# Two-layer attention network on one core: the last network's weights split earlier, and GpSimd's sums in whole slots

## The chip, the cores and the metric

The kernel runs on one core of one Trainium2 chip. The time is the device time of one execution in microseconds (us), and the figure shown for a kernel is the median of its runs. The core has five engines that take their instructions in order, each from its own queue: PE (TensorE, matmuls; its weight loads are shown apart as PEld), DVE (VectorE), ACT (ScalarE), POOL (GpSimd) and SP (SyncE, which here only issues transfers). They wait for each other by semaphores: an instruction adds to one when it is done, and another engine's queue stands at a wait until the count is reached.

## The reference, cut to what matters

Two layers, each an attention times a gate, on 2 sequences of 1024 tokens with 128 features. The change lies in the second layer.

```python
# layer 2: x is (2, 1024, 128), 16 heads of 64
xn = rms_norm(layernorm(x), gamma)
q, k, v = split(xn @ w_qkv)
attn = softmax(q @ k.T * 64**-0.5)          # per head
s = concat(attn @ v) @ w_out
h = silu((ln @ w1) * s1) * ((ln @ w2) * s2) # "last network", 512 wide; ln = layernorm(x)
h = gelu((h @ h1) * sh1)
h = gelu((h @ h2) * sh2)
x = x + s * silu((h @ w3) * s3)
```

## The kernel before

**The second attention** runs in 16 steps, m = 0 to 15. A step is one sequence and one pair of heads. It has 16 slots: two halves of 512 queries, and in each half 8 tiles of 128 keys. A slot works on both heads of the pair, so its probabilities `prob` are 128x1024 (two heads by 512 queries). Slots come in batches b = 0 to 7 of two. PE makes the scores of a slot (`st_ps`, lines 1691 to 1703), ACT takes the exponential into one of 6 `prob` buffers (L1862), PE multiplies it with the values (`o_ps`, L1719). The kernel also needs the sum of the probabilities over the keys: POOL adds slot after slot into `acc` (L2053), one operation for each head, 7 slots of each half (the first slot is an operand of the second). The two operations of a slot are independent of each other; each waits only for the same head's operation of the slot before.

When a half's sums are complete, DVE transposes them (`turned`, L1952) and reduces them (`den_part`, L1959), PE and ACT sum over partitions (`den_out`), DVE takes the reciprocal and spreads it (`rden`, L1967) and multiplies the half's output with it (`o_n`, L1975, an operation with both inputs in SBUF). PE then projects `o_n` (`pj_ps`, L1624) and DVE adds the result to `y` (L1915). `o_n` of a step's second half is made in batch 5 of the next step, that of the first half in batch 7 of its own. Between these DVE takes the row maxima of the next step (`mx_part`, L1924 and L1927), which frees the PSUM banks into which PE writes the next products.

**The order** of each engine is written out by hand in the functions `tensor`, `scalar`, `vector`, `gpsimd` of `second_attention` (called for every m and b, or every slot) and in the blocks at the end of `two_layers`. After step 15 the calls with m = STEPS (16) finish it: PE has its last values' products (slots 14, 15), then the last network begins.

**The last network** uses fp32 operands split into a high and a low part. Its weights are 14 tiles: m1 and m2 (128x512 each), four of h1, four of h2 (128x512), four of m3 (128x128). `scalar_split` makes the high part on ACT (L2226), `gpsimd_split` the low part on POOL (L2231). The raw weights are loaded by SP (`sync_raw`) behind step 3. `splits_at` says which tile is split when: one tile in each of steps 8 to 13 (in batch 4 on ACT, behind slot 9 on POOL), and the other 8 in step 15, where POOL does them behind its last slot. The high parts lie over `xr`, the tokens of the attention's projections, so that half of them can be made only when the first sequence is through and half only when the last projection is done; the input's split (`x_hi`, `x_lo`) is done in step 15 too, on POOL behind slot 10.

## Time and profile before

| | |
|---|---|
| median of 2 runs | 1076.24 us (1076.05 to 1076.44) |
| the profiled execution's own time | 1075.95 us |
| its span, first to last instruction | 1074.2 us |
| PE busy in the span | 1042.9 us, 97% |
| POOL busy | 822.9 us, 77% |
| DVE busy | 801.8 us, 75% |
| ACT busy | 564.3 us, 53% |
| PE of the 40 slices of the span, busy tenths | 9 in all but two: slice 35 has 4, the last 8 |
| chain that ended last, by engine | PE 74%, DVE 11%, POOL 6%, issue 5%, ACT 3% |

The whole-span shares hide the stages. The second attention's steps run from about 300 to 925 us, the last network from about 945 us to the end. A timeline row is a run of like instructions on one engine: start, duration, line, names, shapes, count, and in brackets how long the engine was idle before it and what released it. A record of POOL can begin shortly before the one ahead of it has ended.

### The profile page before, as it was taken

What the parts mean: (1) busy time and instruction counts of PE and PEld (TensorE: products, weight loads), DVE (VectorE), ACT (ScalarE), POOL (GpSimd) and SP (SyncE); (2) the same over time, 40 slices, a digit from 0 to 9 for tenths busy, and PEclk for the clock granted to TensorE, in tenths of its full rate; (3) what the DMA queues carried; (4) which work ended last, traced back from release to release, by engine and by line L of the source; (5) the groups of instructions that cost most, each with busy time, mean ns of one, the idle gap of its engine ahead of it and who ended that gap; (6) DMA issues with size and microseconds to landing.
All of it is one profiled execution on the core that took longest, in us unless ns stands there. A gap on an engine that the chain in (4) does not pass through costs nothing.

```text
span 1074.2 us, 22406 instructions
## 1 busy us (share of the span) xinstructions
PE 1042.9 (97%) x8784; PEld 666.2 (62%) x8784; DVE 801.8 (75%) x1235; ACT 564.3 (53%) x912; POOL 822.9 (77%) x742
## 2 busy tenths in 40 slices
PE   9999999999999999999999999999999999499998
PEld 7898898777645545545554545555554554167886
DVE  4657866577767878878888887888787886965553
ACT  4634453556565555556555565555555555334442
POOL 5778997755469999999999999999999999900000
PEclk9999999999999999999999999999999999799999
DMA  7423234543000000300000000000000000000000
GB/s 231 140 81 100 85 121 125 163 133 115 23 1 2 1 2 1 108 1 1 2 1 1 2 1 1 2 1 1 2 1 2 1 2 1 0 1 10 10 1 20
DMA packets 32681, 40.24 MB, mean 37 GB/s; under 512 B 4544, under 2 KB 24384, under 8 KB 31296
## 3 DMA queue, kind: packets, MB, share of 16 engines
q1 hardware_dynamic: 32256, 38.80, 11.0%
q8 instruction: 70, 1.15, 0.4%
q14 instruction: 35, 0.29, 0.1%
q10 hardware_dynamic: 320, 0.01, 0.0%
HBM read 28.97 MB, written 9.70 MB: 36 GB/s over the span
## 4 chain that ended last, share of the span: by engine, by line
PE 74%; DVE 11%; POOL 6%; issue 5%; ACT 3%; SPq 0%; DMA 0%; DVEq 0%; POOLq 0%; ACTq 0%
PE o_ps L1719 15%; PE mx_ps L1672 6%; PE ha_banks L641 4%; PE st_ps L1691 4%; PE st_ps L1697 4%; PE st_ps L1694 4%; POOL acc L2053 4%; PE bank L2142 4%; PE bank L2143 3%; PE bank L2144 3%; PE pj_ps L1624 2%; PE mx_ps L1604 2%; PE mx_ps L1609 2%; DVE o_n L1975 2%; DVE mx_part L1924 2%
## 5 line engine op out<-in xcount | busy, mean ns | idle before, releaser
L2053 POOL TENSOR_TENSOR acc<-acc,prob 128x512 f32<-128x512 f32 x384 | 491.2, 1320 | 9.3 <-ACT prob L1862 9.3
L1862 ACT ACTIVATE prob<-st_ps 128x1024 f32<-128x1024 f32 x256 | 248.4, 1022 | 208.5 <-PE st_ps L1697 106.6
L1719 PE MATMUL o_ps<-prob,v_cur 128*64 128x512 f32 x1024 | 244.8, 599 | 0.0
L1924 DVE TENSOR_REDUCE mx_part<-mx_ps 128x1 f32<-128x512 f32 x258 | 168.2, 679 | 28.5 <-PE mx_ps L1672 17.5
L1719 PEld LDWEIGHTS o_ps<-prob,v_cur 128*64 128x64 f32 x1024 | 69.6, 137 | 122.1 <-issue 82.4
L1927 DVE TENSOR_REDUCE mx_part<-mx_ps 128x2 f32<-128x1024 f32 x78 | 95.5, 1225 | 45.4 <-PE mx_ps L1672 45.3
L1672 PE MATMUL mx_ps<-k_hi,q_hi 64*128 64x512 f32 x414 | 112.0, 456 | 2.5 <-DVE mx_part L1927 0.4
L1697 PE MATMUL st_ps<-q_hi,d_lo 64*128 64x512 f32 x512 | 101.8, 390 | 0.0
L2053 POOL TENSOR_TENSOR acc<-prob 128x512 f32<-128x512 f32 x64 | 80.9, 1285 | 26.1 <-ACT prob L1862 26.1
L1672 PEld LDWEIGHTS mx_ps<-k_hi,q_hi 64*128 64x128 f32 x414 | 47.0, 183 | 84.2 <-issue 51.2
L949 POOL TENSOR_TENSOR ha_wide<-ha_pt,ha_own 128x512 f32<-128x512 f32 x64 | 74.5, 1188 | 9.2 <-ACT ha_pt L905 9.1
L1691 PE MATMUL st_ps<-q_hi,d_hi 64*128 64x512 f32 x384 | 76.9, 392 | 0.0
L1694 PE MATMUL st_ps<-q_lo,d_hi 64*128 64x512 f32 x384 | 76.4, 390 | 0.0
L1975 DVE TENSOR_TENSOR o_n<-o_sum,rden 128x512 f32<-128x512 f32 x32 | 60.4, 1888 | 0.1
L1924 DVE TENSOR_REDUCE mx_part<-pj_ps 128x1 f32<-128x512 f32 x86 | 58.4, 679 | 0.0
L1697 PEld LDWEIGHTS st_ps<-q_hi,d_lo 64*128 64x128 f32 x512 | 49.0, 184 | 10.3
L2260 ACT ACTIVATE whole<-bank,cols 128x512 f32<-128x512 f32 x32 | 22.0, 688 | 61.9 <-PE bank L2144 61.9
L1624 PE MATMUL pj_ps<-o_n,wo 128*64 128x512 f32 x128 | 33.9, 609 | 15.5 <-DVE o_n L1975 15.5
L1604 PE MATMUL mx_ps<-xr,w_raw 128*64 128x512 f32 x168 | 45.3, 618 | 0.0
L1835 ACT ACTIVATE o_sum<-o_ps 128x512 f32<-128x512 f32 x32 | 19.2, 600 | 47.5 <-PE o_ps L1719 47.5
L1952 DVE STREAM_TRANSPOSE turned<-acc 128x1024 f32<-128x1024 f32 x32 | 39.5, 1235 | 4.8 <-POOL acc L2053 4.8
L861 ACT ACTIVATE ha_q<-ha_banks,ha_head_bq 128x128 f32<-128x128 f32 x128 | 35.5, 377 | 12.5 <-PE ha_banks L641 12.5
(392 smaller groups left out, 2159.4 us busy)
## 6 DMA issues: line engine op xcount, KB each, us to landing
w_tile<-w_rows SPq DMA_DIRECT2D x72, 128.0 KB, 3.0
v_rows<-ha_v SPq DMA_DIRECT2D x8, 1024.0 KB, 4.1
ha_vt<-v_rows SPq DMA_DIRECT2D x16, 512.0 KB, 4.1
q_max<-mx_turned SPq DMA_DIRECT2D x128, 1.0 KB
h_w<-in_h SPq DMA_DIRECT2D x2, 1024.0 KB, 8.3
w_raw<-in_w SPq DMA_DIRECT2D x8, 192.0 KB, 3.9
head_wkv<-in_wkv SPq DMA_DIRECT2D x2, 512.0 KB, 4.8
m_w<-in_m SPq DMA_DIRECT2D x3, 256.0 KB, 3.0
```

Source lines behind the costliest of these rows:

```text
L949: d = pool.tensor_tensor(wide[r][:, seq, :, :, :], t.unsqueeze(3).to_broadcast([P, G // 2, HEADS, GROUPS]), own[:, :].unsqueeze(1).unsquee ...
L1604: mm = pe.matmul(to[rows(h), :], w_raw[:, p, of], xr[:, chunk(q, half), :], start=True, stop=True, skip_group_check=True)
L1672: mm = pe.matmul(to[h], q_hi[q % 2][rows(h), tile(i)], k_hi[q % 2][rows(h), half_of(keys)], start=True, stop=True)
L1691: pe.matmul(st[:, h, :], upper[rows(h), :], qh[rows(h), half_of(half)], start=fresh, stop=False, skip_group_check=True)
L1694: pe.matmul(st[:, h, :], upper[rows(h), :], ql[rows(h), half_of(half)], start=False, stop=False, skip_group_check=True)
L1697: mm = pe.matmul(st[:, h, :], dl[rows(h), tile(j)], qh[rows(h), half_of(half)], start=False, stop=not fresh, skip_group_check=True)
L1719: mm = pe.matmul(o_ps[rows(h), :], v_cur[:, m % 2, j, rows(h)], prob[:, (16 * m + slot) % RING, h, :], start=(j == 0), stop=(j == KT - 1), ...
L1862: act.activation(prob[:, n % RING, :, :], st_ps[:, slot % 2, :, :], ACT.Exp, scale=SCALE).then_inc(s_exp, 1)
L1924: dve.reduce_max(mx_part[:, h, i, keys:keys + 1], maxima_banks(q, n)[h], AX_X).then_inc(s_mxr, 1)
L1927: dve.reduce_max(mx_part[:, :, i, keys:keys + 1], both, AX_X).then_inc(s_mxr, 1)
L1975: dve.tensor_tensor(o_n[:, half, :], o_sum[:, half, :], rden[:, half, :], ALU.mult).then_inc(s_on, 1)
L2053: pool.tensor_tensor(total, old, new, ALU.add).then_inc(s_acc, 1)
```

## The change

1. POOL adds both heads of a slot in one 128x1024 operation (was two of 128x512). It now waits for the operation of the slot before, its immediate predecessor, and counts 2 on `s_acc`.
2. In step 15 POOL stops after slot 11. The last four slots are added by DVE, in `vector_add`, behind DVE's work of step 15.
3. In step 15 POOL waits, before slot 10, until `s_on` has reached 30, that is until DVE has made `o_n` of step 14's second half.
4. The high parts of the weights lie in free memory. So the splits run one tile a step from step 3 (steps 3 to 12), the four small tiles of m3 together in step 13, and none in step 15. SP loads the raw weights behind step 1 (was 3).
5. The input's split moves to step 14: batch 2 on ACT, behind slot 7 on POOL. The waits for the projections go.

```diff
+    BY_VECTOR = 12
...
+    def vector_add(dve, slot):
+        dve.wait_ge(s_exp, 16 * (STEPS - 1) + slot + 1)
+        dve.wait_ge(s_acc, 2 * (ADDS * (STEPS - 1) + 7 + slot - KT - 1))
+        dve.tensor_tensor(acc[:, 1, :, :], acc[:, 1, :, :], prob[:, (16 * (STEPS - 1) + slot) % RING, :, :], ALU.add)\
+           .then_inc(s_acc, 2)
...
-        if j == 0:
+        if j == 0 or m == STEPS - 1 and slot >= BY_VECTOR:
             return
+        if (m, slot) == (STEPS - 1, BY_VECTOR - 2):
+
+            pool.wait_ge(s_on, 2 * m)
         if j == 1 and m:
             pool.wait_ge(s_turns, den_done(m - 1, half, "turned"))
         pool.wait_ge(s_exp, 16 * m + slot + 1)
-        for h in range(2):
-            new, total = prob[:, (16 * m + slot) % RING, h, :], acc[:, half, h, :]
-            old = prob[:, (16 * m + slot - 1) % RING, h, :] if j == 1 else total
-            if j > 1:
-                pool.wait_ge(s_acc, 2 * (ADDS * m + 7 * half + j - 2) + h + 1)
-            pool.tensor_tensor(total, old, new, ALU.add).then_inc(s_acc, 1)
+        new, total = prob[:, (16 * m + slot) % RING, :, :], acc[:, half, :, :]
+        old = prob[:, (16 * m + slot - 1) % RING, :, :] if j == 1 else total
+        if j > 1:
+            pool.wait_ge(s_acc, 2 * (ADDS * m + 7 * half + j - 1))
+        pool.tensor_tensor(total, old, new, ALU.add).then_inc(s_acc, 2)
...
-            act.wait_ge(t2.s_pj, t2.V_HALF)
-        if i == EARLY:
-            act.wait_ge(t2.s_pj, t2.V_END)
...
-        LOADED = 3
+        LOADED = 1
...
-        SPLIT_END = 4
+        FIRST_SPLIT, WIDE = 3, end.TILES - HT
         def splits_at(m, b):
-            if m == END:
-                return [end.EARLY + 2 * b, end.EARLY + 2 * b + 1] if b < SPLIT_END else []
-            return [m - PAIRS] if b == 4 and 0 <= m - PAIRS < end.EARLY else []
+            n = m - FIRST_SPLIT
+            if b != 4 or not 0 <= n <= WIDE:
+                return []
+            return [n] if n < WIDE else range(WIDE, end.TILES)
...
-                        if m == END and b == SPLIT_END:
+                        if (m, b) == (END - 1, 2):
                             end.scalar_x(act)
...
+                for slot in range(t2.BY_VECTOR, 16):
+                    t2.vector_add(dve, slot)
                 t2.vector(dve, STEPS, 0)
...
-                        if m == END and slot == 2 * SPLIT_END + 2:
+                        if (m, slot) == (END - 1, 7):
                             end.gpsimd_x(pool)
-                        if m < END and slot % 2:
+                        if slot % 2:
                             for i in splits_at(m, slot // 2):
                                 end.gpsimd_split(pool, i)
-                for i in range(end.EARLY, end.TILES):
-                    end.gpsimd_split(pool, i)
```

On POOL, the end of its queue: step 15 and what follows, in the kernel before (`acc<-prob` is a half's first add, `h_lo` and `m_lo` are weight splits, `x_lo` the input's).

```order
L2053 TENSOR_TENSOR acc<-prob 128x512 x2
L2053 TENSOR_TENSOR acc<-acc,prob 128x512 x12
L2053 TENSOR_TENSOR acc<-prob 128x512 x2
L2053 TENSOR_TENSOR acc<-acc,prob 128x512 x2
L2277 TENSOR_TENSOR x_lo<-xn,x_hi 128x512
L2053 TENSOR_TENSOR acc<-acc,prob 128x512 x10
L2231 TENSOR_TENSOR h_lo<-h_w,h_hi_200 128x512
```

Three more `h_lo` and the four `m_lo` of m3 follow it.

The same place after the change: steps 14 (from its first half's last adds) and 15.

```order
L2063 TENSOR_TENSOR acc<-acc,prob 128x1024 x6
L2277 TENSOR_TENSOR x_lo<-xn,x_hi 128x512
L2063 TENSOR_TENSOR acc<-prob 128x1024
L2063 TENSOR_TENSOR acc<-acc,prob 128x1024 x2
L2044 TENSOR_TENSOR d_lo<-d_all,d_hi 128x768
L2063 TENSOR_TENSOR acc<-acc,prob 128x1024 x4
L2063 TENSOR_TENSOR acc<-prob 128x1024
L2063 TENSOR_TENSOR acc<-acc,prob 128x1024 x6
L2063 TENSOR_TENSOR acc<-prob 128x1024
L2063 TENSOR_TENSOR acc<-acc,prob 128x1024 x2
```

The eight splits behind step 15 are gone, `x_lo` is in step 14, and POOL's work ends with slot 11.

On DVE, from `den_part` of step 15's batch 5 to the last network's first operation, before.

```order
L1959 TENSOR_REDUCE den_part<-turned 128x32
L1975 TENSOR_TENSOR o_n<-o_sum,rden 128x512
L1965 RECIPROCAL den_rcp<-den_out 128x16
L1967 STREAM_TRANSPOSE rden<-den_rcp 128x512
L1975 TENSOR_TENSOR o_n<-o_sum,rden 128x512
L1915 TENSOR_TENSOR y<-pj_ps,y 128x512
L2301 SCALAR_TENSOR_TENSOR whole_217<-bank,cols,sgm_244 128x512
```

The same place after the change (line 1982 is the new add).

```order
L1960 TENSOR_REDUCE den_part<-turned 128x32
L1976 TENSOR_TENSOR o_n<-o_sum,rden 128x512
L1966 RECIPROCAL den_rcp<-den_out 128x16
L1968 STREAM_TRANSPOSE rden<-den_rcp 128x512
L1976 TENSOR_TENSOR o_n<-o_sum,rden 128x512
L1982 TENSOR_TENSOR acc<-acc,prob 128x1024 x4
L1916 TENSOR_TENSOR y<-pj_ps,y 128x512
L2301 SCALAR_TENSOR_TENSOR whole_217<-bank,cols,sgm_244 128x512
```

Only the row with the four adds is new; they stand between the second `o_n` and `y`. PE's order is the same in both kernels.

## Rows read from the trace of the kernel before

**Rows 1.** Windows: stretch, its length; busy us (count) by engine; PE clock; DMA
```profile
core 0: us, PE busy (x) PEld busy (x) DVE busy (x) ACT busy (x) POOL busy (x), PEclk, DMA share, GB/s
430.00:480.00 50.00, 49.73 (x330) 25.59 (x328) 42.15 (x64) 27.05 (x37) 47.99 (x38) 1.00 0.17 59
...
547.39:586.94 39.55, 39.41 (x268) 20.28 (x266) 33.58 (x50) 22.06 (x29) 37.47 (x30) 1.00 0.01 1
...
744.11:783.66 39.55, 39.41 (x267) 20.29 (x266) 32.29 (x50) 22.51 (x30) 38.73 (x31) 1.00 0.01 1
...
925.10:945.60 20.50, 4.98 (x12) 1.39 (x12) 17.63 (x5) 0.91 (x2) 14.82 (x15) 0.58 0.00 1
945.60:1000.00 54.40, 54.40 (x239) 42.62 (x238) 33.61 (x55) 24.32 (x38) 0.00 (x0) 1.00 0.02 6
```

**Rows 2.** Chain that ended last, in order of time: the same instruction, a step apart
```profile
547.12 1.25 DVE mx_part L1924 x2
...
586.66 1.25 DVE mx_part L1924 x2
```

**Rows 3.** Timeline of PE at the end of step 15 and after
```profile
923.15 1.94 PE L1719 MATMUL o_ps<-prob,v_cur 128*64 128x512 f32 x8
940.62 1.98 PE L1624 MATMUL pj_ps<-o_n,wo 128*64 128x512 f32 x4 [15.53 <-DVE o_n L1975]
...
945.62 0.50 PE L2142 MATMUL bank<-x_hi,m_hi 128*128 128x512 f32 x1
...
951.31 1.08 PE L1624 MATMUL pj_ps<-o_n,wo 128*64 128x512 f32 x4
```

**Rows 4.** Timeline of DVE, same stretch
```profile
915.24 1.25 DVE L1952 STREAM_TRANSPOSE turned<-acc 128x1024 f32<-128x1024 f32 x1 [4.83 <-POOL acc L2053]
...
917.66 22.82 DVE L1975 TENSOR_TENSOR o_n<-o_sum,rden 128x512 f32<-128x512 f32 x1
...
941.51 0.69 DVE L1975 TENSOR_TENSOR o_n<-o_sum,rden 128x512 f32<-128x512 f32 x1
...
947.45 0.75 DVE L2301 SCALAR_TENSOR_TENSOR whole<-bank,cols,sgm 128x512 f32<-128x512 f32 x1 [4.06 <-ACT sgm L2249]
```

**Rows 5.** Timeline of POOL, step 15 and its splits
```profile
897.72 2.52 POOL L2053 TENSOR_TENSOR acc<-prob 128x512 f32<-128x512 f32 x2
900.19 14.94 POOL L2053 TENSOR_TENSOR acc<-acc,prob 128x512 f32<-128x512 f32 x12
...
938.19 1.74 POOL L2231 TENSOR_TENSOR m_lo<-m_w,m_hi 128x128 fp32r<-128x128 f32 x4
```

**Rows 6.** Timeline of DVE in batches 5 to 7 of step 6
```profile
565.51 1.33 DVE L1975 TENSOR_TENSOR o_n<-o_sum,rden 128x512 f32<-128x512 f32 x1
...
568.48 0.69 DVE L1924 TENSOR_REDUCE mx_part<-mx_ps 128x1 f32<-128x512 f32 x1 [0.34 <-PE pj_ps L1672]
...
573.60 1.68 DVE L1975 TENSOR_TENSOR o_n<-o_sum,rden 128x512 f32<-128x512 f32 x1
576.42 1.23 DVE L1927 TENSOR_REDUCE mx_part<-mx_ps 128x2 f32<-128x1024 f32 x1 [1.15 <-PE mx_ps L1672]
```

**Rows 7.** Timeline of POOL, step 6, slot 10
```profile
563.78 5.45 POOL L2053 TENSOR_TENSOR acc<-acc,prob 128x512 f32<-128x512 f32 x4 [0.64 <-ACT prob L1862]
```

**Rows 8.** Lines by form, POOL: names, shapes, count, busy us, mean ns, idle before
```profile
L2053 POOL TENSOR_TENSOR acc<-acc,prob 128x512 f32<-128x512 f32 x384 | 491.2, 1320 | 9.3 <-ACT prob L1862 9.3
...
L2036 POOL TENSOR_TENSOR d_lo<-d_all,d_hi 128x768 fp32r<-128x768 f32 x16 | 29.2, 1828 | 1.6 <-ACT d_hi L1829 1.6
...
L985 POOL TENSOR_TENSOR head_wkv_lo<-head_wkv,head_wv_hi 128x1024 fp32r<-128x1024 f32 x1 | 2.4, 2393 | 4.9 <-ACT head_wv_hi L884 4.9
```

**Rows 9.** Timeline of POOL: L481 waits for the completion of L477, its predecessor
```profile
35.71 0.22 POOL L477 CAST wc_hi<-wc_raw 128x32 fp32r<-128x32 f32 x1
36.01 0.46 POOL L481 TENSOR_TENSOR wg_lo<-wg_raw,wg_hi 128x128 fp32r<-128x128 f32 x1
```

**Rows 10.** Lines by form, DVE: a two-input operation on 256 columns
```profile
L1902 DVE TENSOR_TENSOR d_lo<-pj_ps,k_hi 128x256 fp32r<-128x256 f32 x15 | 6.4, 424 | 15.0 <-ACT k_all L1811 15.0
```

**Rows 11.** Timeline of ACT: the last exponentials of step 15
```profile
922.57 1.94 ACT L1862 ACTIVATE prob<-st_ps 128x1024 f32<-128x1024 f32 x2 [1.51 <-PE st_ps L1697]
```

More of the change, by code:

```diff
@@ L2061, in second_attention @@
     s.vector_normalize = vector_normalize
+    s.vector_add, s.BY_VECTOR = vector_add, BY_VECTOR
     s.vector_start, s.gpsimd_start, s.gpsimd_begin = vector_start, gpsimd_start, gpsimd_begin
@@ L2065, in second_attention, with last_network @@
     s.s_osum, s.s_out = s_osum, s_out
-    s.V_END, s.V_HALF = count_of[STEPS - 1, ("v", 1)], count_of[PAIRS - 1, ("v", 1)]
+    s.V_END = count_of[STEPS - 1, ("v", 1)]
     s.ADDS_END, s.MXR_END = 2 * ADDS * STEPS, MXR_END
     return s
-def last_network(nc, c, e, t2, a, x, xn, out, raw, at, token_places, weight_place, pair_place, raw_place, late_place):
+def last_network(nc, c, e, t2, a, x, xn, out, raw, at, free_place, spare_place, weight_place, pair_place, raw_place, late_place):
     s = Const()
-    w_hi = {"h1": [token_places[i // 2][0].sb(f"h1_hi{i}", [P, HID], F32R) for i in range(HT)],
-            "h2": [token_places[i // 2][1].sb(f"h2_hi{i}", [P, HID], F32R) for i in range(HT)],
-            "m1": [token_places[2][0].sb("m1_hi0", [P, HID], F32R)], "m2": [token_places[2][0].sb("m2_hi0", [P, HID], F32R)],
-            "m3": [token_places[2][1].sb(f"m3_hi{i}", [P, P], F32R) for i in range(HT)]}
+    w_hi = {n: [free_place.sb(f"{n}_hi{t}", [P, size], F32R) for t in range(of)] for n, (of, size) in MLP_W.items() if n != "h2"}
+    w_hi["h2"] = [spare_place.sb(f"h2_hi{t}", [P, HID], F32R) for t in range(HT)]
     w_lo = {n: weight_place.sb(n + "_lo", list(t.shape), F32R) for n, t in raw.items()}
-    x_hi, x_lo = (pair_place.sb(n, [P, CH], F32R) for n in ("x_hi", "x_lo"))
+    x_hi, x_lo = (spare_place.sb(n, [P, CH], F32R) for n in ("x_hi", "x_lo"))
     RING = 3
@@ L2104, in last_network @@
     cut_by = {n: max(i for i, (of, _) in enumerate(tiles) if of == n) + 1 for n in raw}
-    EARLY = cut_by["h1"]
     USES = 2 * HT + 2 * HT
@@ L2269, in scalar_x @@
     def scalar_x(act):
-        act.wait_ge(t2.s_pj, t2.V_END)
-        act.wait_ge(t2.s_st, 16 * (STEPS - 1))
         act.activation(x_hi[:, :], xn[:, 0, HALO:], ACT.Copy).then_inc(s_xhi, 1)
@@ L2335, in vector_last @@
             dve.tensor_tensor(fin[:, of], x[:, k, of], res[:, of], ALU.add).then_inc(s_fin, 1)
-    s.TILES, s.EARLY = len(tiles), EARLY
+    s.TILES = len(tiles)
     s.sync_raw, s.sync_out = sync_raw, sync_out
@@ L2404, in two_layers @@
         WEIGHTS = late.at
-        token_places = [[Region(nc, XR + 8 * KB * i + 4 * KB * half) for half in range(2)] for i in range(3)]
-        end = last_network(nc, c, e, t2, a, x, xn, out, raw, at, token_places, Region(nc, WEIGHTS), Region(nc, HEAD + 56 * KB),
-                           Region(nc, HEAD + 91 * KB), Region(nc, FIRST))
+        end = last_network(nc, c, e, t2, a, x, xn, out, raw, at, Region(nc, XR + 8 * KB), Region(nc, pairs.at), Region(nc, WEIGHTS),
+                           Region(nc, HEAD + 56 * KB), Region(nc, HEAD + 91 * KB), Region(nc, FIRST))
         BATCHES, TURNS = t2.BATCHES, head.TURNS
```

## The prediction

> **What bounds the kernel now.** I read the page first (PE busy almost throughout, one thin slice near the end), then the windows, the chain, and the timelines of three engines at the thin slice. A step takes 39.54 us: the same DVE instruction of the chain comes back after 586.66 - 547.12 [rows 2]. In such a step PE is busy 39.41 of 39.55 us, so the attention is paced by PE, and POOL, with 37.47 us in a step without a split and 38.73 us in one with a split, follows closely behind it [rows 1]. Behind 945.6 us PE is busy without a break [rows 1]. The one hole is between: from 925.1 to 945.6 us PE is busy 4.98 of 20.50 us [rows 1]. It waits 15.53 us for `o_n` of step 14's second half, then starts again slowly: the projection takes 1.98 us where the same four matmuls take 1.08 us at 951.31 [rows 3]. The granted clock of that stretch is 0.58 on average, between the two levels of 1.2 and 2.4 GHz, and 1.00 behind it [rows 1].
>
> Why is `o_n` late? The operation is not waiting for data that comes late in POOL's work; it is recorded as running, for 22.82 us, where the same operation takes 0.69 us at 941.51 [rows 4]. It starts at 917.66 and ends at 940.48. POOL has a record at every moment from 897.72 on and ends at 939.93, 0.55 us earlier [rows 5]. So I read it as DVE standing at a port that POOL never lets go. In step 6 the same operation takes 1.33 and 1.68 us [rows 6]: there POOL gives way after the add that is running. The difference in step 15 is that POOL runs behind and has its whole queue ready. Its consecutive records overlap: 14 adds take 897.72 to 915.13, 1.24 us each, less than one's mean duration of 1.32 us [rows 5, 8].
>
> **The change part by part.**
>
> *The hole.* PE's last products of slots 12 and 13 run 923.15 to 925.09, then comes the projection of `o_n`, then the products of slots 14 and 15, then the last network, which started at 945.62 [rows 3]. If `o_n` is there in time, this is 1.94 + 1.08 + 1.94 us behind 923.15, less about 0.1 us that rows overlap: the network starts at 928.05. That gives 945.62 - 928.05 = 17.57 us, the idle time of 15.53 us and 2.0 us of slow clock. PE's order is unchanged and it is busy throughout behind that, so the shift is carried to the end, unless DVE or POOL is late for it.
>
> *When is `o_n` ready?* First the price of a double add on POOL. The trace has one POOL operation of two inputs on 1024 columns, 2.39 us; 512 columns take 1.32 us with waits in it and 768 take 1.83 us [rows 8], so 1024 by the slope from 512 to 768 is 2.34 us. I take 2.39. The new wait for its own predecessor costs a gap: where POOL waits so already, one record ends at 35.93 and the next begins at 36.01, 0.08 us [rows 9]. So a slot costs 2.47 us, against 14.94/6 = 2.49 us for its two adds before [rows 5]: merging neither gains nor loses. The bound below is 2.34 + 0.08 = 2.42, above two single durations and the gap, 2 x 1.32 + 0.08 = 2.72 us.
>
> In step 15 the first half's sums start at 897.72 [rows 5]; `x_lo`, new in step 14, finds some 2 us of idle time there. They end at 897.72 + 2.39 + 6 x 2.47 = 914.9 us (915.1 before). DVE reaches `o_n` 2.42 us after it begins to transpose them (917.66 - 915.24 [rows 4]), at 917.4. POOL does slot 9 until 917.3 and then stands at the new wait for `s_on`. Behind it in POOL's queue are slots 10 and 11 only. So the port is free, `o_n` takes 0.69 us and is done by 918.2, 6.9 us before PE wants it at 925.09.
>
> *The last four slots.* POOL does slots 10 and 11 from 918.3 to 923.2, or 923.9 if DVE's second `o_n` slips in between. DVE's adds have two inputs of 1024 columns, which no row shows. 256 columns take 0.42 and 512 take 0.69 us [rows 10, 4], so 1024 by the slope take 1.23 us; the bound above is POOL's 2.39 us. I take 1.23, the same engine's slope, and 0.08 us for each wait: 4 x 1.31 = 5.2 us, to 929.1 us. The probabilities are there at 924.5 [rows 11]. DVE's `y` add ends at 929.8, and its first operation of the last network, at 947.45 before [rows 4], is wanted at 929.88. It just fits. With 2.39 us an add the chain would be 4.6 us late. That DVE is late by less than a microsecond costs nothing; the rest would go into the time, so up to 4 us for this bound.
>
> *The splits.* Ten of the fourteen tiles now run in steps 3 to 12, one each, a window in which PE has no hole to hide them. POOL pays 38.73 - 37.47 = 1.26 us a step [rows 1], inside the 39.55 us that PE takes, and in steps like that at 744.11 PE was busy as before. What ACT pays hides in an engine that is busy 22.51 of 39.55 us [rows 1]. The cover on POOL is thin: 39.55 - 38.73 = 0.82 us. If a slot cost more than 2.49 + 0.82/14 = 2.55 us, POOL would become the pace. Removing the splits behind step 15 is worth nothing by itself beyond the hole: they lay behind POOL's last add, and it is the port that they held.
>
> *The load* moves past two steps of small `q_max` transfers on SP's queue. Before, it fell into 430 to 480 us at 59 GB/s, and PE was busy 49.73 of 50 us there [rows 1]. Nothing.
>
> *DVE's waits in every step.* A double add holds the port up to 2.39 us instead of 1.32 us. Here the Trainium skill speaks against the change, and the rows must be weighed. In batch 5, POOL's slot 10 starts at 563.78 because it waits for ACT [rows 7], so it ends at 566.17; `o_n` wants in at 565.51 and would be done at 566.17 + 0.69 = 566.86, as before (566.84 [rows 6]). Then slot 11 to 569.3, the 768 columns to 571.1, slots 12 and 13 to 573.5 and 576.0. `o_n` of batch 7 wants in at 573.60 [rows 6]: at worst it is done at 576.7, where the next product was ready at 576.42 [rows 6], 0.3 us late. In a step with a split POOL is 1.3 us later and this `o_n` is done at about 574.7. So between 0 and 0.3 us in each of 4 or 5 steps: I take 0.
>
> The rule is in "SBUF — State Buffer", section "Who interferes with whom": a VectorE operation with two SBUF inputs and a GpSimd operation that reads SBUF exclude each other, and whichever is second blocks until the first has finished. By it, doubling the operation doubles the longest wait, and at the bound of 2.39 us for each of 30 `o_n` one would lose tens of microseconds; by the rows above the waits fall where there is slack. The rule doesn't cover 22.82 us behind adds of 1.3 us, so row and rule differ there. "GPSIMD Engine Reference", section "2. Architecture", adds that GpSimd's cores begin the next instruction when their own share is done, unless it waits for completion; no row shows the cores, but the overlapping records agree.
>
> **The sum.** 1075.95 (the profiled execution) - 17.57 = 1058.4 us. The median of the runs shown is 0.29 us above that execution: 1058.7 us.
>
> **The rivals.**
>
> *A. As summed*, 1056 to 1062 us: 0.74. PE is full before and behind the hole, so there is little else to gain; the few microseconds above are DVE's adds or small stalls.
>
> *B. POOL becomes the pace* (the other side). From 2.55 us a slot each excess is paid 14 times in 11 steps with a split: 15.4 us for 0.1 us. All of the gain is gone at 2.66 us, and the kernel is slower than before beyond. At the bound of 2.72 us it is 14 x 0.17 x 11 = 26 us there, 14 x 0.09 x 4 = 5 us in the steps without a split (whose limit is 2.63 us), so 1058.7 + 31 = 1090 us. For: the cover is 0.82 us a step. Against: three POOL rows lie on one slope, and the gap has a row. 0.10 for 1062 to 1076, 0.03 above 1076.
>
> *C. DVE's longer waits stall PE in every step.* If PE were stalled by 0.3 to 0.6 us in each of 30 `o_n`, 9 to 18 us: 1068 to 1076 us. For: 0.34 us of idle time is all DVE has behind `o_n` in batch 5 [rows 6]. Against: POOL's add there is anchored by ACT [rows 7]. 0.07.
>
> *D. The hole stays.* If DVE never waits for more than the POOL operation that is running, `o_n` would have ended by 917.66 + 1.32 + 0.69 = 919.7 us, so something else held it, the change doesn't touch it, and PE waits as before: 1076 us. This is what the Trainium skill's rule of "SBUF — State Buffer" would mean here. Against: the end 0.55 us behind POOL's last record. 0.03.
>
> *E. More than the hole*, under 1054.7 us: PE would have to gain in the steps, where it idles 0.14 us of each. 0.03.
>
> **How the numbers follow.** A is the likeliest. The range takes in the bound of DVE's adds (+4), the 0.3 us stalls (+1.5) and the near part of B and C: 1055 to 1066 us. A change of 2% is 21.5 us, about what a measurement of this kernel can tell from none; 1054.7 us is faster by that. E gives faster 0.03, the far end of B slower 0.02, the rest 0.95 within.
>
> **What would show it.** PE's wait for `o_n` of 15.53 us gone, and no row of it over 2 us; the clock 1.00 through 925 to 946; no `o_n` over 3 us; POOL's add of 1024 columns at 2.3 to 2.45 us with gaps of 0.08; the step at 39.54 us in steps 3 to 13; DVE's four adds at 1.23 us. A longer step in 3 to 12 would mean B; a longer step with POOL idle would mean C; an `o_n` of many microseconds at the end would mean D.

## The result and the profile after

| | before | after |
|---|---|---|
| median of 2 runs | 1076.24 us | 1057.96 us (1057.54 to 1058.38) |
| ratio to before, with its 95% interval | | 0.984 [0.982, 0.985] |
| the profiled execution's own time | 1075.95 us | 1057.54 us |
| its span | 1074.2 us | 1055.8 us |

The change takes 18.3 us, 1.6%, off the kernel. The forecast was 1058.7 us, 0.7 us above the median. The page of after, its busy times and two lines of its 40 slices:

```profile
span 1055.8 us, 22183 instructions
...
PE 1039.9 (98%) x8784; PEld 664.3 (63%) x8784; DVE 787.9 (75%) x1239; ACT 563.9 (53%) x912; POOL 784.2 (74%) x514
...
PE   9999999999999999999999999999999999999998
...
PEclk9999999999999999999999999999999999999999
```

The slice with a 4 is gone. The windows of after (stretch, length, busy us and count of each engine, granted clock, DMA share, GB/s): two steps with a split, the last 20.5 us ahead of the last network, and its first 54.4 us. They answer to [rows 1].

```profile
547.39:586.94 39.55, 39.41 (x266) 20.30 (x266) 32.81 (x50) 22.50 (x31) 36.89 (x17) 1.00 0.01 1
744.11:783.66 39.55, 39.41 (x268) 20.22 (x266) 32.84 (x50) 22.51 (x30) 36.91 (x16) 1.00 0.01 1
...
906.70:927.20 20.50, 19.88 (x113) 8.13 (x111) 11.13 (x13) 11.23 (x14) 14.84 (x7) 1.00 0.00 1
927.20:981.60 54.40, 54.40 (x239) 42.65 (x238) 35.50 (x58) 24.32 (x38) 0.00 (x0) 1.00 0.02 6
```

PE is busy 19.88 of the last 20.50 us, where it was busy 4.98 of 20.50 us, and the granted clock is 1.00, the upper level of 2.4 GHz, where it was 0.58. PE's timeline at that place (start, duration, names, idle time before), against [rows 3]:

```profile
922.75 1.94 PE L1720 MATMUL o_ps<-prob,v_cur 128*64 128x512 f32 x8
924.52 1.03 PE L1625 MATMUL pj_ps<-o_n,wo 128*64 128x512 f32 x4
925.37 1.89 PE L1720 MATMUL o_ps<-prob,v_cur 128*64 128x512 f32 x8
927.19 0.50 PE L2149 MATMUL bank<-x_hi,m_hi 128*128 128x512 f32 x1
```

The projection stands behind the products without a wait and takes 1.03 us, where it waited 15.53 us and took 1.98. DVE in the same stretch, against [rows 4]:

```profile
914.83 1.25 DVE L1953 STREAM_TRANSPOSE turned<-acc 128x1024 f32<-128x1024 f32 x1 [4.68 <-POOL acc L2063]
...
917.24 0.68 DVE L1976 TENSOR_TENSOR o_n<-o_sum,rden 128x512 f32<-128x512 f32 x1
...
919.22 1.77 DVE L1976 TENSOR_TENSOR o_n<-o_sum,rden 128x512 f32<-128x512 f32 x1
923.36 5.30 DVE L1982 TENSOR_TENSOR acc<-acc,prob 128x1024 f32<-128x1024 f32 x4 [2.37 <-POOL acc L2063]
928.58 0.68 DVE L1916 TENSOR_TENSOR y<-pj_ps,y 128x512 f32<-128x512 f32 x1
929.18 0.74 DVE L2301 SCALAR_TENSOR_TENSOR whole<-bank,cols,sgm 128x512 f32<-128x512 f32 x1
```

`o_n` takes 0.68 us, not 22.82. POOL, against [rows 5]: the last add of the first half (slot 7), slot 9, the wait for `s_on`, then slots 10 and 11:

```profile
912.33 2.39 POOL L2063 TENSOR_TENSOR acc<-acc,prob 128x1024 f32<-128x1024 f32 x1 [0.17 <-POOL acc L2063]
914.68 2.37 POOL L2063 TENSOR_TENSOR acc<-prob 128x1024 f32<-128x1024 f32 x1
918.06 2.38 POOL L2063 TENSOR_TENSOR acc<-acc,prob 128x1024 f32<-128x1024 f32 x1 [1.01 <-DVE o_n L1976]
920.61 2.62 POOL L2063 TENSOR_TENSOR acc<-acc,prob 128x1024 f32<-128x1024 f32 x1 [0.17 <-POOL acc L2063]
```

Where the time came from, by the trace: from the first product of `q_max` (297.80 us before, 297.17 after) to the last network's first matmul (945.62 and 927.19) it is 647.82 us before and 630.02 after, 17.80 us less. The other 0.6 us lie ahead of 297 us, where the change moves none of POOL's or DVE's work. From the last network's first matmul to the end it is 128.6 us in both.

### The profile page after: what moved, and what is told of

Same layout as the page of the kernel before. It is cut to its first block, busy times and chain, and to the rows that moved or that the text cites. A ratio compares the mean times of both kernels' runs of the same rounds, so it can differ in the third digit from the quotient of the medians.

```text
span 1055.8 us, 22183 instructions
## 1 busy us (share of the span) xinstructions
PE 1039.9 (98%) x8784; PEld 664.3 (63%) x8784; DVE 787.9 (75%) x1239; ACT 563.9 (53%) x912; POOL 784.2 (74%) x514
## 4 chain that ended last, share of the span: by engine, by line
PE 80%; DVE 8%; POOL 3%; issue 3%; ACT 3%; DMA 1%; SPq 1%; DVEq 0%; POOLq 0%; ACTq 0%
PE o_ps L1720 18%; PE mx_ps L1673 7%; PE st_ps L1692 5%; PE st_ps L1698 5%; PE st_ps L1695 5%; PE ha_banks L641 5%; PE bank L2149 4%; PE bank L2151 3%; PE bank L2150 3%; PE mx_ps L1610 3%; PE pj_ps L1625 3%; PE mx_ps L1605 3%; PE ha_banks L694 2%; PE ha_banks L705 2%; DVE mx_part L1925 2%
## 5 line engine op out<-in xcount | busy, mean ns | idle before, releaser
L2063 POOL TENSOR_TENSOR acc<-acc,prob 128x1024 f32<-128x1024 f32 x188 | 456.5, 2428 | 34.2 <-POOL acc L2063 23.7
L2063 POOL TENSOR_TENSOR acc<-prob 128x1024 f32<-128x1024 f32 x32 | 76.6, 2393 | 23.6 <-ACT prob L1863 23.6
L1976 DVE TENSOR_TENSOR o_n<-o_sum,rden 128x512 f32<-128x512 f32 x32 | 42.5, 1328 | 0.1
L894 ACT ACTIVATE ha_o<-ha_banks 128x512 f32<-128x512 f32 x32 | 19.1, 598 | 43.0 <-PE ha_banks L694 42.3
L1695 PEld LDWEIGHTS st_ps<-q_lo,d_hi 64*128 64x128 f32 x384 | 36.9, 184 | 7.6
```

The source lines that it names most:

```text
L1695: pe.matmul(st[:, h, :], upper[rows(h), :], ql[rows(h), half_of(half)], start=False, stop=False, skip_group_check=True)
L2063: pool.tensor_tensor(total, old, new, ALU.add).then_inc(s_acc, 2)
```

## Experiments

The question behind all of them: what exactly held `o_n` for 22.82 us, and which part of the change lets it go? "Locked out" below means a record of `o_n` that lasts over several of POOL's operations. "The port" is, as in the prediction, what such an operation of DVE (two inputs in SBUF) and one of POOL can't hold at once; the runs show the waiting, not the part of the chip. "Let in" is the moment at which DVE gets it, and a "handover" is one such moment while POOL has work ready. In all seven locks below `o_n` ends 0.55 us behind the end of a POOL record.

### One part of the change at a time

**Merging alone** (part 1), in the kernel before:

```diff
-        for h in range(2):
-            ...
-            if j > 1:
-                pool.wait_ge(s_acc, 2 * (ADDS * m + 7 * half + j - 2) + h + 1)
-            pool.tensor_tensor(total, old, new, ALU.add).then_inc(s_acc, 1)
+        if j > 1:
+            pool.wait_ge(s_acc, 2 * (ADDS * m + 7 * half + j - 1))
+        pool.tensor_tensor(total, old, new, ALU.add).then_inc(s_acc, 2)
```

> The kernel before with part 1 alone: one double add for each slot on GpSimd, waiting for the slot before; it still adds all slots of step 15 and splits eight weight tiles behind them. Theory P (VectorE gets the shared port only when GpSimd's next operation has not yet begun, so a wait for the predecessor's completion lets it in after at most one operation): o_n of step 14's second half takes under 3.1 us, the hole at 925 us is gone and the last network starts near 927 us. The port is then contended further on: VectorE's two-input operations act00lo to act03lo (from about 931 us) meet GpSimd's last adds and its splits, which don't wait for each other and run to about 942 us. TensorE waits there in the first hidden layer, about 7 us and 1 to 2 us of slow clock: 1065 to 1068 us. Theory L (only the operation that is running is waited for; the 22.8 us have another cause): hole unchanged, 1076 us. Theory I (only a long idle time of GpSimd lets VectorE in, a gap of 0.17 us doesn't): o_n again lasts until GpSimd's queue ends, about 942 us: 1077 to 1079 us.

Measured 1060.13 us (1059.89 to 1060.48), ratio 0.986 [0.984, 0.987]: 15.5 us less than the kernel before, run beside it (1075.68 us), so this part alone brings most of the gain, and more than the 1065 to 1068 us expected. DVE and POOL of this kernel at the request:

```profile
917.10 0.68 DVE L1975 TENSOR_TENSOR o_n<-o_sum,rden 128x512 f32<-128x512 f32 x1
```

```profile
914.54 2.37 POOL L2052 TENSOR_TENSOR acc<-prob 128x1024 f32<-128x1024 f32 x1
917.08 2.95 POOL L2052 TENSOR_TENSOR acc<-acc,prob 128x1024 f32<-128x1024 f32 x1 [0.17 <-POOL acc L2052]
...
934.27 6.56 POOL L2230 TENSOR_TENSOR h_lo<-h_w,h_hi 128x512 fp32r<-128x512 f32 x4
```

The merged add waits for its predecessor's completion, so POOL has a gap of 0.17 us before nearly every add. `o_n` asks at 917.10, 0.02 us behind the start of the add that follows such a gap, and takes its undisturbed 0.68 us; that add is stretched from 2.38 to 2.95 us. My expectation missed in what follows: the splits (from 934.27 on, four without a gap between them) were to lock DVE out again, and they don't: DVE's `act01lo`, the longest, takes 2.21 us, and PE waits 1.6 us in all for `act01lo` to `act03lo`.

**The splits and the input's split moved alone** (parts 4 and 5; POOL adds head by head to the end, without a wait):

```diff
-        LOADED = 3
+        LOADED = 1
-        SPLIT_END = 4
+        FIRST_SPLIT, WIDE = 3, end.TILES - HT
...
-                for i in range(end.EARLY, end.TILES):
-                    end.gpsimd_split(pool, i)
```

> The kernel with parts 4 and 5 alone: single adds on GpSimd in all slots, no wait for the port, no adds on VectorE, but the weight splits in steps 3 to 13 and the input's split in step 14. Theory P: o_n still stands at the port, from 917.7 us until GpSimd's last add ends, which is now near 932.2 us (939.9 less eight splits of 6.6 us and the input's 1.1 us). The hole shrinks by 7.7 us: 1068 to 1069 us. Theory L: no change, 1076 us. Theory that the splits were what held VectorE and not the adds: hole gone, 1058 us.

Measured 1067.69 us (1067.16 to 1069.12), 0.993 [0.991, 0.995], 0.3 us under the 1068 to 1069 us expected. DVE and the end of POOL:

```profile
916.95 15.24 DVE L1976 TENSOR_TENSOR o_n<-o_sum,rden 128x512 f32<-128x512 f32 x1
```

```profile
914.40 2.50 POOL L2061 TENSOR_TENSOR acc<-prob 128x512 f32<-128x512 f32 x2
916.87 14.78 POOL L2061 TENSOR_TENSOR acc<-acc,prob 128x512 f32<-128x512 f32 x12
```

`o_n` is still locked out, until 932.19, and POOL's last add ends at 931.65: again 0.55 us earlier. So it isn't the splits that hold the port, but whatever POOL has in its queue without a break. Moving the eight splits and the input's away shortens the lock by about what they took, 22.82 - 15.24 = 7.6 us.

**The port wait alone** (part 3):

```diff
+        if (m, slot) == (STEPS - 1, 10):
+            pool.wait_ge(s_on, 2 * m)
```

> The kernel before with part 3 alone: GpSimd waits before slot 10 of step 15 until o_n of step 14's second half is made. Theory P and theory I: that o_n takes 0.7 to 1.4 us and PE's wait of 15.5 us at 925 us is gone. GpSimd then runs without a gap to about 940.6 us, so VectorE stands at the port once more, in the second o_n (from 919.6 us) or in act00lo (from 931 us), and TensorE waits either for the projection of that o_n (from 934 us) or in the first hidden layer: 1066 to 1070 us. Theory L: o_n's wait had another cause, but whatever it was the new wait makes GpSimd stand for it too, so the hole is there or longer: 1076 to 1090 us.

Measured 1064.12 us, but spread (1062.21, 1067.71, 1066.02, 1059.29), 0.990 [0.986, 0.993]. In the profiled execution, 1062.21 us, step 15's `o_n` takes 0.68 us, as it should. But there is a new lock at another place, in the first of the 16 steps:

```profile
335.10 6.69 DVE L1975 TENSOR_TENSOR o_n<-o_sum,rden 128x512 f32<-128x512 f32 x1
```

The same `o_n` takes 1.76 us in the kernel before, and nothing of the edit is near it. PE waits 3.0 us for the maxima behind it. That is most of the distance to 1059.2 us (below); the two slowest executions have no trace, and what they lost in is open. At the end of step 15 my expectation (1066 to 1070 us, DVE locked out once more) missed: the second `o_n` takes 0.69 us, and `act00lo` is let in within POOL's gapless run:

```profile
933.93 1.51 DVE L2290 TENSOR_TENSOR act00lo<-whole,act00hi 128x512 fp32r<-128x512 f32 x1
```

### What lets a waiting VectorE in?

Two theories were left. **G:** it needs a gap in POOL's work behind its request. **Phi:** it depends on the moment within a POOL operation at which it asks: it is locked out within 0.13 us behind the start of an add (0.12 us in before). A third, **T**, came out of the runs: it depends on how long POOL has worked without a break when it asks.

**Real waits for the predecessor in three slots** of step 15, in the kernel before:

```diff
-            if j > 1:
+            if m == STEPS - 1 and slot in (9, 10, 11):
+                pool.wait_ge(s_acc, 2 * (ADDS * m + 7 * half + j - 1) + h)
+            elif j > 1:
```

> The kernel before; single adds stay, but in step 15 each of the six adds of slots 9, 10 and 11 also waits for the completion of its immediate predecessor. No operation is larger and no work is moved. Theory P: o_n is let in at the end of the add that is running, so it takes under 2.1 us and the hole at 925 us is gone; GpSimd's end moves from 939.9 to about 941 us, and VectorE's act00lo (from 931 us) now stands at the port until then, with everything queued behind it, so that TensorE waits in the first hidden layer from about 935 to 942 us: 1066 to 1069 us. Theory L and theory I: hole unchanged, 1076 to 1078 us.

Measured 1059.25 us (1059.21 to 1059.39), 0.985 [0.983, 0.986]. Six stricter waits, no operation changed, give nearly the whole gain: `o_n` takes 0.83 us. I had expected later operations of DVE to be locked out by POOL's gapless rest, and they are not: `act00lo` at 931.0 is let in after 1.65 us with no gap in POOL around it. G alone doesn't explain that, nor the steady steps of before, where `o_n` is let in at 565.51 within four adds without a gap [rows 6, 7].

**Gaps only behind the request.** The same, with the stricter wait only in the second add of slot 10 and in slot 11:

```diff
+            if m == STEPS - 1 and (slot == 10 and h == 1 or slot == 11):
```

> The kernel before; the wait for the immediate predecessor's completion only in the second add of slot 10 and the two of slot 11 of step 15, which are behind the moment at which VectorE asks (917.66 us, 0.124 us behind the start of slot 10's first add). So the place of the request is as before and only the gaps behind it are new. Theory G, and Phi joined with G (a VectorE that is locked out gets in at the first gap): o_n is let in at 918.9 us and takes about 1.8 us: 1059 to 1061 us. If a gap of 0.08 us doesn't help a VectorE that is locked out already: o_n lasts until GpSimd's queue ends at about 941 us: 1077 us.

Measured 1059.15 us (1058.77 to 1060.49), 0.984 [0.980, 0.987]. DVE and POOL:

```profile
917.02 1.72 DVE L1975 TENSOR_TENSOR o_n<-o_sum,rden 128x512 f32<-128x512 f32 x1
```

```profile
914.46 2.50 POOL L2055 TENSOR_TENSOR acc<-prob 128x512 f32<-128x512 f32 x2
916.93 2.96 POOL L2055 TENSOR_TENSOR acc<-acc,prob 128x512 f32<-128x512 f32 x2
```

`o_n` asks 0.09 us behind the start of an add, much as in before (0.12 us), after the same history, and gets the port at the first gap, 0.08 us wide, at 918.27. So one such gap frees a VectorE that would be locked out.

**Asking later.** In before, small maxima over `acc` on DVE ahead of this `o_n` shift its request: to 0.30 us behind an add's start (one of 128 columns), or to 0.04 us behind the start of a later one (512, 232 and 232 columns). Nobody reads them.

```diff
+        if (m, b) == (STEPS - 1, 5):
+            for i, size in enumerate((128,)):       # or (512, 232, 232)
+                dve.reduce_max(mx_part[:, 0, i, 0:1], acc[:, 0, 0, 0:size], AX_X)
```

> The kernel before, nothing changed on GpSimd; one small VectorE operation (the maximum over 128 columns of acc, whose result nobody reads) is put ahead of the o_n of step 15's batch 5, so that VectorE asks for the port about 0.2 us later. Theory Phi (VectorE is locked out only when it asks within about 0.13 us behind the start of a GpSimd operation that overlapped its predecessor: in the kernel before it asks 0.124 us behind such a start, in the kernel with only the splits moved 0.088 us; at 0.134 us and more it was let in each time): it now asks 0.3 us behind the start and is let in at that operation's end, o_n takes about 1.5 us, no hole at 925 us: 1059 to 1061 us. Theory G (only a gap between two GpSimd operations lets it in): o_n again lasts until 940 us: 1076 to 1077 us.

> As ask_later_0_2, but with three such operations over 512, 232 and 232 columns, about 1.21 us in all: one GpSimd add (1.24 us) later, so that VectorE asks at the same place behind the start of the next add, about 0.1 us. Theory Phi: locked out again, o_n lasts until 940 us: 1075 to 1078 us. If asking later were what helps, whatever the place: 1060 us, as with 0.2 us. The place is met only to some 0.03 us; at 0.13 us or more behind the start Phi too says 1060 us, so the trace's own distance decides.

Measured 1075.33 us, ratio 1.000 [0.998, 1.001], and 1075.73 us, 0.999 [0.998, 1.001]. `o_n` of the two kernels:

```profile
917.01 22.61 DVE L1975 TENSOR_TENSOR o_n<-o_sum,rden 128x512 f32<-128x512 f32 x1
```

```profile
919.23 21.62 DVE L1975 TENSOR_TENSOR o_n<-o_sum,rden 128x512 f32<-128x512 f32 x1
```

At 0.30 us as at 0.04 us it stays locked out to the end of POOL's queue. Phi, with its 0.13 us, falls. A later moment of the 1.24 us from one add to the next was not tried here. One of the 10 executions of the first kernel took 1080.71 us, and one of the 19 of the kernel before, run beside it, 1082.39 us; what these two lost in is open.

**A gap only ahead of the request**, 2 us or 17 us before it: only the first add of slot 9, or only that of slot 2, waits for its predecessor.

```diff
+            if m == STEPS - 1 and slot == 9 and h == 0:      # or slot == 2
```

> The kernel before; one single wait is stricter: in step 15 the first add of slot 9 waits for the completion of its immediate predecessor, which makes one gap in GpSimd's work at about 915 us, some 2.5 us ahead of VectorE's request, and none behind it. Theory T (what counts is how long GpSimd has run without a break when VectorE asks: in all traces so far a request up to 8.1 us behind the last break was let in, at 10.5 us 7 of 8, at 26.6 to 27.8 us none unless a gap followed): o_n is let in at the end of the add that is running and takes 1.2 to 2.0 us, no hole: 1059 to 1061 us. Theory G (only a gap behind the request helps): o_n lasts until GpSimd's end at 940 us: 1075 to 1077 us. Later requests (act00lo, about 931 us, some 16 us behind that gap) may be locked out by T, which would cost several us in the first hidden layer: then up to 1070 us.

> As gap_ahead_2us, but the one stricter wait is at the first add of slot 2, some 17 us ahead of the request. A measurement between the two ranges of theory T (let in up to 11.8 us, locked out from 26.6 us): let in gives 1059 to 1065 us, locked out 1075 to 1077 us. T expects the lock-out to be likelier than not; theory G expects 1076 us.

2 us ahead: 1059.24 us in the median, 0.985 [0.983, 0.987]; one of the five executions, the profiled one, took 1064.95. In it `o_n` asks at 923.12, 2.35 us behind the gap, and is let in at the end of the running add, though POOL has no gap after the request:

```profile
923.12 0.71 DVE L1975 TENSOR_TENSOR o_n<-o_sum,rden 128x512 f32<-128x512 f32 x1
```

```profile
905.66 14.94 POOL L2055 TENSOR_TENSOR acc<-acc,prob 128x512 f32<-128x512 f32 x12
920.77 2.51 POOL L2055 TENSOR_TENSOR acc<-prob 128x512 f32<-128x512 f32 x2 [0.17 <-POOL acc L2055]
923.24 2.98 POOL L2055 TENSOR_TENSOR acc<-acc,prob 128x512 f32<-128x512 f32 x2
```

G falls: a gap before the request does as well. The lock at the first step is in this execution too: `o_n` takes 6.72 us at 336.64, PE waits 3.2 us, and the way to the second `o_n` behind it is 4.8 us longer than in before (381.26 - 336.64 against 375.85 - 336.02), with a granted clock of 0.88 from 336 to 350 us. That is most of the 5.7 us between this execution and the others. `act00lo` asks 10.7 us behind the last handover here and is let in:

```profile
936.92 1.29 DVE L2290 TENSOR_TENSOR act00lo<-whole,act00hi 128x512 fp32r<-128x512 f32 x1
```

17 us ahead: 1076.92, 1058.81, 1075.83 and 1075.99 us. This kernel has two outcomes, locked out three times and let in once; in the profiled one `o_n` takes 22.79 us. A median of these says nothing, so no ratio is given.

Taken together, over the two-SBUF-input operations of DVE in all traces, by the time since POOL's last break (an idle time, a gap behind a wait, or the end of the POOL operation at an earlier handover) at the moment that DVE asks:

| time since POOL's last break | outcome |
|---|---|
| up to 8.1 us | let in, always (all `o_n` of the steady steps, the last network's) |
| 10.5 us (first step, nine kernels with single-head adds) | let in 7 times (1.73 to 1.76 us), locked out twice (6.69, 6.72 us) |
| 10.7 us (`gap_ahead_2us`, `act00lo`) and 11.8 us (`port_wait_only`, `act00lo`) | let in, once each |
| about 17.4 us (`gap_ahead_17us`) | locked out in the traced execution; by the times let in 1 of 4 |
| 26.6 to 27.8 us, no gap behind | locked out in 4 of 4 traces |
| the same, with a gap behind (`gaps_behind_the_request`) | let in at the gap |

That fits T, as a chance that falls with the time, not as a limit: at 10.5 us both outcomes occur, with requests 0.07 to 0.10 us behind the start of an add in either case. T isn't wholly parted from the moment of asking: all seven locks have requests 0.04 to 0.30 us behind the start of an add, while the two `act00lo` at 10.7 and 11.8 us asked 0.56 and 0.35 us behind one. The cause of T is open. One idea is that consecutive adds come to overlap more the longer POOL runs on, until no moment between them is free. The traces speak against it as far as records can: in before the overlap of consecutive records does grow, from 0.04 us at 898 us to 0.07 us at 917 us, but in `splits_moved_only` it is 0.03 us at the request and in `gap_ahead_17us` 0.04 us, and DVE is locked out all the same. The locks of 6.7 us also end inside a gapless run of POOL, 0.55 us behind the end of an add, and why there is open. In the steady steps of before POOL stands idle for ACT once or twice a step and hands over at each `o_n`, so no request comes later than 8.1 us behind a break. In step 15 PE has no maxima to make for a next step, the slots come faster than POOL adds, and POOL's last break is the handover at 891 us.

### One part of the change taken back

**Without the port wait** (after, part 3 out):

```diff
-        if (m, slot) == (STEPS - 1, BY_VECTOR - 2):
-
-            pool.wait_ge(s_on, 2 * m)
```

> The changed kernel without part 3, GpSimd's wait for s_on before slot 10 of step 15. GpSimd's double adds have a gap of 0.17 us between them. By G and by Phi the o_n of step 14's second half, asked for at 917.2 us, is let in at the end of the add that is running or in the gap, and is done by 920.2 us at the latest, 4 us before TensorE wants it: 1057.5 to 1058.5 us, as with the wait. If only the explicit wait opens the port: o_n lasts until GpSimd's last add ends at about 922 us, still before 924.5 us, so the time is the same and only the row of o_n (over 4.5 us) would tell.

Measured 1057.79 us (1057.54 to 1058.91), 0.982 [0.979, 0.985]: the same as after. `o_n`, and POOL's operation beside it:

```profile
917.44 0.68 DVE L1976 TENSOR_TENSOR o_n<-o_sum,rden 128x512 f32<-128x512 f32 x1
```

```profile
917.42 2.94 POOL L2060 TENSOR_TENSOR acc<-acc,prob 128x1024 f32<-128x1024 f32 x1 [0.17 <-POOL acc L2060]
```

The merged adds already have the gap that lets DVE in. Part 3 is worth nothing beside part 1.

**Without the sums on VectorE** (after, part 2 out, the port wait kept at slot 10):

```diff
-    BY_VECTOR = 12
+    BY_VECTOR = 16
```

> The changed kernel without part 2: GpSimd adds slots 12 to 15 as well (it still waits for s_on before slot 10), so its queue ends at about 933.5 us instead of 923. Its double adds have gaps, so VectorE's act00lo to act03lo (from 931 us) are let in, each after up to 2.4 us. TensorE waits for them in the first hidden layer by 0 to 3 us: 1058 to 1061 us. If the adds by VectorE were what made the gain possible: above 1065 us.

Measured 1058.27 us (1058.15 to 1058.47), 0.984 [0.983, 0.986]. POOL ends at 933.8 us, `act01lo` takes 2.06 us, and PE waits 0.29 us for `act02lo`. So part 2 is worth about 0.3 us by that wait; the times (1058.15 to 1058.47 against 1057.54 to 1058.38 us) overlap and don't show it by themselves.

**POOL with more work**: after, and one add of 512 columns more in each of steps 1 to 14, behind slot 4, into memory that nobody reads.

```diff
+        if slot in EXTRA and 0 < m < STEPS - 1:         # EXTRA = (4,)
+            pool.wait_ge(s_wo, 16 * PAIRS)
+            pool.tensor_tensor(scratch[:, :], ..., ALU.add)
```

> The changed kernel with one more GpSimd operation in each of steps 1 to 14, behind slot 4: an add of 512 columns into a tile that nobody reads, about 1.24 us. It prices the cover on GpSimd. In a step with a split it is idle 2.6 us in gaps over 0.15 us, of which 12 x 0.17 = 2.0 us are its own waits, so 0.6 us are left: if GpSimd then becomes the pace, 0.65 us for each of the 11 steps with a split, about 7 us: 1063 to 1067 us. If the prob buffers and VectorE's slack absorb it: 1058 us.

Measured 1059.06 us (1058.5 to 1061.05), 0.985 [0.984, 0.987], not the 1063 to 1067 us of a POOL that sets the pace. The window of the step at 744.11, and POOL around the added operation:

```profile
744.11:783.66 39.55, 39.41 (x266) 20.30 (x264) 32.90 (x50) 22.52 (x30) 38.03 (x18) 1.00 0.01 1
```

```profile
747.52 2.37 POOL L2068 TENSOR_TENSOR acc<-acc,prob 128x1024 f32<-128x1024 f32 x1 [0.17 <-POOL acc L2068]
749.84 1.30 POOL L2071 TENSOR_TENSOR scratch<-wo 128x512 f32<-128x512 f32 x1
751.08 2.38 POOL L2068 TENSOR_TENSOR acc<-acc,prob 128x1024 f32<-128x1024 f32 x1
```

The step is as long as before. The added operation costs only 751.08 - 750.06 = 1.02 us, since it stands in the gap that the next add would have waited (to 747.52 + 2.37 + 0.17 = 750.06). In after, POOL has 0.91 us of idle time at the split of that step, and here that is gone: POOL now has no idle time but its own gaps in that step, and its first add of the step's first half starts up to 0.1 us later behind its probabilities than in after. So the cover is used up and the step just holds. The profiled execution's span is 1.6 us longer than that of after (1057.4 against 1055.8). None of it lies in the steps: 0.77 us lie ahead of 298 us, 0.6 us in PE's wait for `den_part` in step 15 (1.22 us, against 0.62), and 0.3 us in the last network.

## Why the prediction was right

- **The hole, held and mis-sized by 0.2 us.** Forecast 17.57 us, found 17.80. (The rows as forecast, 1.94 + 1.08 + 1.94 - 0.1, make 4.86 us; the sum was carried on with 4.9.) The network was to start 4.9 us behind the last products of slots 12 and 13, and starts 927.19 - 922.75 = 4.44 us behind them: the three rows are 0.10 us shorter in all and overlap by 0.42 us, not by 0.1. Against it stands 0.23 us lost between 297 us and there, about the size of one step that is longer (39.84 us against 39.55, below). The 0.6 us ahead of the attention are nothing that the change did.
- **The cause of the late `o_n`, held.** I took it from two numbers: an operation of 0.69 us recorded as 22.82, and its end 0.55 us behind POOL's last record. With POOL's queue shortened (`splits_moved_only`) it ended 0.55 us behind the new end, 7.6 us less in duration. Rival D, that something else held it, is out, and `gaps_behind_the_request` shows it the other way round: nothing but three of POOL's waits was changed, and `o_n` took 1.72 us.
- **When it is ready, held.** First half's sums done at 914.72 (forecast 914.9), `o_n` asks at 917.24 (917.4) and is done at 917.92 (918.2).
- **But why it is let in was half wrong.** I put it on the new wait for `s_on`. That wait does hold POOL (1.01 us), but without it the result is the same; it is the wait for the predecessor, 0.17 us at each add, that does it, and it does so from the first part of the change on. I had priced that wait as a cost only.
- **The price of a slot, mis-sized.** The add itself was right: 2.37 to 2.39 us (2.39). The gap behind the own predecessor is 0.17 us, not the 0.08 of [rows 9]. The size of that row's operation, a 128x32 cast, doesn't explain it: between adds of 512 columns the gap is 0.08 us too, where the new wait stands alone (the second add of a slot), and 0.14 to 0.17 us where the wait for the exponential stands ahead of it, as it does in every merged add. A slot takes 2.55 us, not 2.47. That stands exactly at the limit that I gave rival B (2.55 us), and POOL did not become the pace. The limit was too tight for two reasons. The 2.49 us of before were those of step 15; in a steady step a slot of before took (37.47 - 1.83)/14 = 2.55 us (1.83 us are the 768-column operation), since each handover to `o_n` stretches an add. And in after not all 14 slots pay the gap: behind a split, behind the 768-column operation and in front of a half's first add there is none. POOL of after in the step at 547.39, by form (busy us, mean ns, idle before and its releasers):

```profile
L2063 POOL TENSOR_TENSOR acc<-acc,prob 128x1024 f32<-128x1024 f32 x13 | 31.6, 2432 | 1.9 <-POOL acc L2063 1.5 <-ACT prob L1863 0.3
L2063 POOL TENSOR_TENSOR acc<-prob 128x1024 f32<-128x1024 f32 x2 | 4.8, 2400 | 1.0 <-ACT prob L1863 1.0
L2044 POOL TENSOR_TENSOR d_lo<-d_all,d_hi 128x768 fp32r<-128x768 f32 x1 | 1.8, 1826 | 0.0
L2234 POOL TENSOR_TENSOR h_lo<-h_w,h_hi 128x512 fp32r<-128x512 f32 x1 | 1.3, 1278 | 0.0
```

POOL is busy 36.89 us and stands 1.5 us in its own gaps; nearly all the rest of 39.55 us, 1.2 us, is idle time for ACT, in a step with a split. `after_pool_plus_1_2` showed that about 1.0 us of it can be used.

- **The last four slots, held.** DVE's add of 1024 columns takes 1.23 us, the slope's value, with 0.13 us between them: 5.30 us, from 923.36 to 928.66 (5.2, to 929.1). `y` and the first `whole` follow without a wait and PE has none. That the sums had to leave POOL was not so: with POOL doing them PE loses 0.3 us.
- **The waits of DVE in the steps, held at nothing.** The page's group of all `o_n`, and PE's waits from 830 us to 930 us:

```profile
L1976 DVE TENSOR_TENSOR o_n<-o_sum,rden 128x512 f32<-128x512 f32 x32 | 42.5, 1328 | 0.1
```

```profile
PE pj_ps L1617 <- DVE den_part L1960: 0.6, 1, 0.6
PE pj_ps L1617 <- DVE mx_part L1925: 0.2, 1, 0.2
```

`o_n` takes 1328 ns in the mean. In a step with a split it is 1.65 and 0.68 us, in one without 1.25 and 2.60 us, and the longest is 2.61 us, under the 3 us that I had set. One step is longer: 39.84 us, that behind step 13's four splits of m3, where `o_n` takes 2.08 us at 841.73. The other three kernels with merged adds and these splits have it too, `merge_only` and `splits_moved_only` don't, so it takes both. That it is rival C, 0.3 us once, is likely from the late `o_n`; no wait of PE shows it. Here the row bears out the rule of the Trainium skill, "SBUF — State Buffer", section "Who interferes with whom" (the second of a VectorE operation with two SBUF inputs and a GpSimd operation blocks until the first has finished): in after no `o_n` waited for more than one operation of POOL. Step 15 of before (22.82 us) and the locks of the experiments (6.7 us and more) went far beyond it.
- **The splits and the load, held.** PE is busy 39.41 of 39.55 us in steps with a split, as before. The load now falls into 360 to 390 us, at 85 GB/s, and PE is busy 30.00 of 30.00 us there, as in before.

What would have shown it came as listed: no wait for `o_n`, the clock at 1.00, adds at 2.3 to 2.45 us (but for those stretched by a handover, 2.6 to 2.9), no `o_n` over 3 us; only the gap of 0.08 us was another, and one step was longer by 0.3 us.

## What to carry to other kernels

Where a record of VectorE with two SBUF inputs lasts over several GpSimd operations and ends just behind one, look for the last moment at which GpSimd had a break; a single wait of GpSimd for its own predecessor, placed near the request, can give the port back for 0.1 to 0.2 us. Here one such wait 2 us ahead of the request brought 16.0 us (`gap_ahead_2us`, in the median) and three behind it 16.8 us of the 18.3 us that a change over five places brings; one 17 us ahead of it failed in three of four executions. A wait that looks like pure cost in the sum may be what pays; price the parts one by one before crediting the one that was meant to help.

## What the runs showed of the hardware

- A VectorE operation with two SBUF inputs can be locked out by a gapless run of GpSimd for as long as it lasts: 22.8, 22.6, 21.6 and 15.2 us here. It happened in all four traces in which GpSimd had run 26.6 us or more without a break and had none behind the request, never up to 8.1 us, and in some executions at 10.5 and 17.4 us. A gap of 0.08 us behind the request ended it.
- A handover, where it happens, costs little: VectorE's `o_n` is done 0.55 us behind the end of the running GpSimd operation, and the next one is stretched by about 0.5 us (2.94 and 2.95 against 2.38 us).
- A wait for the completion of the own predecessor leaves a gap of 0.17 us on GpSimd between adds of 1024 columns. Between adds of 512 columns it is 0.08 us in some places (at 918.27 in `gaps_behind_the_request`, where it freed VectorE) and 0.17 us in others (at 920.77 in `gap_ahead_2us`). VectorE's dependent adds of 1024 columns stand 0.13 us apart.
- For GpSimd two adds of 512 columns take 2.49 us without a gap, and one of 1024 takes 2.37 to 2.39 us, 2.55 us with its gap of 0.17.
